# Rebuilding the front of a fused attention and feed-forward kernel on one core

## What is computed

```
x = x + attn_a(layernorm(x))     # q, k, v of width 1024, ONE head, causal softmax, w_o
x = x + ffn(layernorm(x))
x = x + attn_b(layernorm(x))     # 16 heads of 64, causal, own residual and own LayerNorm
x = x + ffn(layernorm(x))        # the same weights
ffn(x): s = x @ Win + bin                       # 64 units
        h = relu(s[..., None] * W1 + b1)        # 16 inner values per unit
        g = sum over the 16 of h * W2, + b2
        out = g @ Wout + bout
```

## Time and profile before

| | |
|---|---|
| median of 3 runs | 880.62 us (879.36 to 883.76) |
| profiled execution | 878.94 us, span 877.1 us |
| busy: TensorE, VectorE, ScalarE, GpSimd | 728.0, 665.4, 573.9, 520.9 us |
| start / front / back | 0 to 40.2 / to 226 / to 877.1 us |
| granted TensorE clock, mean | 0.923 |

### The profile page before, as it was taken

One profiled execution on the slowest core, in us unless ns is written; L12 is line 12 of the kernel. 1 busy time (PEld: TensorE's weight loads), 2 busy tenths in 40 slices (PEclk: granted clock), 3 DMA queues, 4 the chain that ended last, 5 costly groups with the idle time before them and its releaser, 6 DMA issues. The chain is left out here.

```text
span 877.1 us, 21234 instructions
## 1 busy us (share of the span) xinstructions
PE 728.0 (83%) x7592; PEld 523.7 (60%) x7592; DVE 665.4 (76%) x1358; ACT 573.9 (65%) x1575; POOL 520.9 (59%) x496
## 2 busy tenths in 40 slices
PE   4376666642689999999999999999999999998842
PEld 3265555532457676766767766766776676676531
DVE  2478888875466668868987996898799689879873
ACT  0257666653367676677777777777777777777633
POOL 2156666462156567766785685667578566766831
PEclk9599778865799999999999999999999999999985
DMA  9011111100079988899898888889889889898820
GB/s 210 23 48 49 49 48 37 48 25 36 25 131 150 152 146 141 147 144 140 143 146 137 150 139 145 145 141 144 138 151 143 142 143 141 151 143 152 147 58 24
DMA packets 367142, 100.29 MB, mean 114 GB/s; under 512 B 347968, under 2 KB 364864, under 8 KB 367040
## 3 DMA queue, kind: packets, MB, share of 16 engines
q1 hardware_dynamic: 363776, 96.86, 64.3%
q10 hardware_dynamic: 3264, 2.10, 0.9%
HBM read 8.73 MB, written 2.10 MB: 12 GB/s over the span
## 5 line engine op out<-in xcount | busy, mean ns | idle before, releaser
L1031 POOL TENSOR_TENSOR prob_hl<-prob,prob_hl 128x768 f16<-128x768 f32 (+1 forms) x192 | 347.5, 1810 | 205.3 <-DVE prob_hl L971 205.1
L942 ACT ACTIVATE prob<-wide,neg_max 128x128 f32<-128x128 f32 (+3 forms) x512 | 264.5, 525 | 155.6 <-DVE neg_max L983 155.5
L983 DVE TENSOR_REDUCE neg_max<-wide 128x2 f32<-128x256 f32 (+3 forms) x256 | 204.3, 819 | 109.9 <-PE wide L860 108.6
L855 PE MATMUL wide<-k_sb,q_sb 64*128 64x128 f32 (+3 forms) x1024 | 190.1, 469 | 0.9 <-ACT k_sb L837 0.8
L971 DVE CAST prob_hl<-prob 128x768 f16<-128x768 f32 (+1 forms) x192 | 155.1, 808 | 0.9 <-DMA prob_t<-prob_hl 0.7
L880 PE MATMUL bank<-v_hi,prob_t 128*128 128x64 f16 x1280 | 132.2, 193 | 15.4 <-DMA prob_t<-prob_hl 13.2
L882 PE MATMUL bank<-v_hi,prob_t 128*128 128x64 f16 x1280 | 132.2, 193 | 0.0
L881 PE MATMUL bank<-v_lo,prob_t 128*128 128x64 f16 x1280 | 132.2, 193 | 0.0
L880 PEld LDWEIGHTS bank<-v_hi,prob_t 128*128 128x128 f16 x1280 | 115.3, 98 | 21.4 <-issue 16.2
L882 PEld LDWEIGHTS bank<-v_hi,prob_t 128*128 128x128 f16 x1280 | 113.9, 98 | 0.0
L881 PEld LDWEIGHTS bank<-v_lo,prob_t 128*128 128x128 f16 x1280 | 113.8, 98 | 0.0
(11 more groups left out here) (190 smaller groups left out, 1427.0 us busy)
## 6 DMA issues: line engine op xcount, KB each, us to landing
prob_t<-prob_hl SPq DMA_TRANSPOSE x384, 3.2
x_next<-in_L_attn_a_in_features SPq DMA_DIRECT2D x8, 256.0 KB, 3.0
x_attn<-in_L_attn_a_in_features SPq DMA_DIRECT2D x8, 256.0 KB, 3.3
x_sb<-x_done SPq DMA_DIRECT2D x8, 256.0 KB, 2.3
y_res<-bn_y SPq DMA_DIRECT2D x8, 256.0 KB, 2.3
out_x<-x_done SPq DMA_DIRECT2D x8, 256.0 KB, 2.6
wq_a<-in_L_attn_a_w_q ACTq DMA_DIRECT2D x1, 512.0 KB, 5.3
wq_b<-in_L_attn_b_Wq SPq DMA_DIRECT2D x1, 512.0 KB, 8.4
```

The costliest lines, as they stand in the source:

```text
L855: pe.matmul(dst[:, h, c:c + m], q[e, i * P:(i + 1) * P], k[e, 0:m], start=(i == UNIT_ROWS[u][0]), stop=False)
L942: last = act.activation(prob_2[s][:, at:at + m], score_banks(p, s)[:, h, c:c + m], ACT.Exp, bias=neg_max[p % 2][:, h, i:i + 1], accum_out= ...
L983: last = dve.tensor_reduce(neg_max[p % 2][:, :, i:i + 1], score_banks(p, s)[:, :, c:c + m], AX.X, ALU.max, negate=True)
L1031: pool.tensor_tensor(prob_hl[u][:, w:2 * w], prob_2[u][:, 0:w], prob_hl[u][:, 0:w], ALU.subtract)\
```

## The change

- **Splits** are gone from the front, except that of `xt_hi` and `xt_lo`. Scores, `at_g`, the weighted values and the feed-forward's first product are single products of 4-byte operands; scores cover only the blocks up to the diagonal. ScalarE copies each operand once.
- **Feed-forward:** units 6 and 7 of each half are no longer summed on VectorE. Their `Relu`s stay; `ffn_out_pe` multiplies them with `w2_out`, which is `wout2` scaled by their `w2`, so the output product is 12 products in place of 4.
- **Order:** the turn of sequence `b - 3` (`bn`) stands on TensorE right behind the scores, ahead of the turning of the probabilities, and on ScalarE ahead of the first copy of these; on VectorE the residual `ffn_x_dve` stands first in the step and `bn`'s statistics behind the first row maximum.
- **Start:** all sequences are loaded once, straight into `x_sb`; the small feed-forward weights are loaded early, `attn_b`'s late. Sequence 0 is turned and its `at_g` made between the foldings. `vo_a` isn't scaled any more.
- **Weights of `attn_b`:** the largest value is found after step 2 (`scale_gpsimd`, an all-reduce over partitions on GpSimd), the scaling stands after step 7, the splits after step 8.
- `x_done`'s and `bn_y`'s copies by DMA are gone, and so is the hardware loop over steps.

The core of the diff:

```diff
+        def weighted_values(pe, u, v):
+
+            for k, (i, j) in enumerate(unit_blocks(u)):
+                last = pe.matmul(UO[:, i * P:(i + 1) * P], at_p_t[u][:, k * P:(k + 1) * P], v[:, j * P:(j + 1) * P],
+                                 start=(j == 0), stop=(j == i))
...
+        def load_tokens(sp, *bs):
+            for b in bs:
+                sp.dma_start(x_sb[:, seq(b), :], x_tiles[:, seq(b), :]).then_inc(sem(f"x_in{b}"), 16)
+
         def prepare_loads_sync(sp):
+            load_tokens(sp, 0)
+            sp.wait_ge(sem("b2_zeroed"), 1)
+            for dst, src in f_loads[:4]:
+                sp.dma_start(dst, src).then_inc(sem(LOADED_F), 16)
+            load_tokens(sp, 1)
+            for dst, src in f_loads[4:]:
+                sp.dma_start(dst, src).then_inc(sem(LOADED_F), 16)
+            load_tokens(sp, 2)
+            sp.wait_ge(sem(LOADED_A), 2 * 16)
+            load_tokens(sp, 3)
             for dst, src in b_loads:
                 sp.dma_start(dst, src).then_inc(sem(LOADED_B), 16)
-            sp.wait_ge(sem("b2_zeroed"), 1)
-            for dst, src in f_loads:
-                sp.dma_start(dst, src).then_inc(sem(LOADED_F), 16)
+            load_tokens(sp, *range(4, B))
 
...
+            pool.wait_ge(sem("const_0"), 7)
             front_gpsimd(pool, -2)
-            pool.wait_ge(sem("largest"), 2)
+            front_gpsimd(pool, -1)
+
+        def scale_gpsimd(pool):
+            pool.wait_ge(sem("largest"), 1)
             pool.partition_all_reduce(largest_all[:, :], largest[:, :], P, bass.bass_isa.ReduceOp.max)\
...
         def prepare_tensor(pe):
+            pe.wait_ge(sem("consts"), 3)
+            attn_turn_tensor(pe, 0)
             pe.wait_ge(sem(LOADED_QK_A), 2 * 16)
             for c in range(OC):
                 last = pe.matmul(bank[0][:, 0:P], wq_a[:, c, :], wk_a[:, c, :], start=(c == 0), stop=(c == OC - 1))
             last.then_inc(sem("qk_a_ps"), 1)
-            pe.wait_ge(sem("consts"), 3)
+            pe.wait_ge(sem("qk_a"), 1)
+            attn_g_tensor(pe, 0)
...
+            pe.wait_ge(sem("vo_a"), 1)
+            attn_v_tensor(pe, 0)
...
+            wait(pe, "f_xt", n + 1)
+            pe.matmul(bk[:, :], win2[:, :, :].rearrange("p a m -> p (a m)"), ffn_x[:, :], start=True, stop=True)\
                 .then_inc(sem("f_s_ps"), 1)
 
         def ffn_out_pe(pe, bk, n):
-            wait(pe, "f_add", J * n + J)
+            wait(pe, "f_relu", J * n + J)
+            wait(pe, "f_add", JA * n + JA)
             for i in range(QB):
-                last = pe.matmul(bk[:, i * P:(i + 1) * P], ffn_g[:, i * P:(i + 1) * P], wout2[:, :],
-                                 start=True, stop=True)
+                t = slice(i * P, (i + 1) * P)
+                pe.matmul(bk[:, t], ffn_g[:, t], wout2[:, :], start=True, stop=False)
+                for j in range(JA, J):
+                    last = pe.matmul(bk[:, t], ffn_relu[:, j % RELUS, t], w2_out[:, j - JA, :], start=False,
+                                     stop=(j == J - 1))
             last.then_inc(sem("f_o_ps"), 1)
...
         def ffn_relu_act(act, n, j):
             if j == 0:
                 wait(act, "f_s", n + 1)
-            wait(act, "f_add", J * n + max(j - RELUS + 1, 0))
+            if j >= RELUS:
+                wait(act, "f_add", JA * n + j - RELUS + 1)
+            elif (j + RELUS) >= JA:
+                wait(act, "f_o_ps", n)
+            else:
+                wait(act, "f_add", JA * (n - 1) + j + RELUS + 1)
...
+            dve.tensor_tensor(x_sb[:, seq(n), :], bk[:, :].rearrange("p (a d) -> p a d", d=P),
+                              ffn_xb[:, n % 2 * QB:(n % 2 + 1) * QB, :], ALU.add)\
                 .then_inc(sem("f_x2"), 1)
...
-                wait(sp, "f_x2", b - 2)
-                sp.dma_start(x_sb[:, seq(b - 3), :], x_done[:, :, :]).then_inc(sem("kept"), 16)
-                sp.wait_ge(sem("consts"), 3)
-                wait(sp, "bn_y", b - 2)
-                sp.dma_start(y_res[:, seq(b - 3), :], b_norm.y[:, :, :]).then_inc(sem("y_res_in"), 16)
-            if holds(b, -3, B - 4):
-                wait(sp, "at_y", b + 3)
-                sp.dma_start(x_next[:, :, :], x_tiles[:, seq(b + 3), :]).then_inc(sem("x_next_in"), 16)
...
-                    scores(pe, SC[u], u, at_g_hi, at_g_lo, at_x_hi, at_x_lo, 0).then_inc(sem("at_s"), 1)
+                    scores(pe, SC[u], u).then_inc(sem("at_s"), 1)
+            if attn_1:
+                wait(pe, "at_g", b + 1)
+                attn_turn_tensor(pe, b + 1)
+            if turn:
+                wait(pe, "bn_y", b - 2)
+                wait(pe, "f_x2", b - 2)
+                transposes(pe, FB, y_res[:, seq(b - 3), :].rearrange("p a d -> p (a d)"), QB)\
+                    .then_inc(sem("bn_xt_ps"), 1)
             if attn_2:
-                wait(pe, "at_p", NU * b + 1)
-                transposes(pe, TR[0], prob[0], len(unit_blocks(0))).then_inc(sem("at_pt"), 1)
+                for u in range(NU):
+                    wait(pe, "at_p", NU * b + u + 1)
+                    wait(pe, "at_pt", NU * b + u - 1)
+                    transposes(pe, TR[u % 2], prob[u], len(unit_blocks(u))).then_inc(sem("at_pt_ps"), 1)
             if attn_1:
...
+                attn_g_tensor(pe, b + 1)
+                attn_v_tensor(pe, b + 1)
+            if ffn_1:
+                ffn_project_pe(pe, SC[2], b - 1, before=[("at_p", NU * (b + 1)) if attn_2 else ("f_s", b - 1)])
             if attn_2:
-                wait(pe, "at_p", NU * b + 2)
...
-            if attn_1:
...
-                wait(pe, "at_x_lo", b + 2)
-                split_product(pe, GX[:, :], qk_a_hi[:, :], qk_a_lo[:, :], at_x_hi[:, :], at_x_lo[:, :])\
-                    .then_inc(sem("at_g_ps"), 1)
...
-                if attn_2:
-                    wait(pe, "at_pt_lo", NU * b + u + 1)
+                for u in range(NU):
...
-                    at = v_at(b)
-                    weighted_values(pe, lambda i: UO[:, i * P:(i + 1) * P], u,
-                                    lambda j: at_v_hi[:, bass.ds(at + j * P, P)],
...
-                if u == 1 and ffn_1:
-
-                    ffn_project_pe(pe, SC[2], b - 1, before=[("at_p", NU * (b + 1)) if attn_2 else ("f_s", b - 1)])
+                    weighted_values(pe, u, at_v[:, b % 2, :]).then_inc(sem("at_pv"), 1)
             if ffn_1:
                 ffn_s_pe(pe, SC[2], b - 1)
-            if turn:
-                wait(pe, "bn_y", b - 2)
-                transposes(pe, FB, b_norm.tokens(), QB).then_inc(sem("bn_xt_ps"), 1)
             if ffn_2:
                 wait(pe, "bn_xt_lo", b - 2)
                 ffn_out_pe(pe, FB, b - 2)
...
-            prob_t_scalar(0)
+            if attn_1:
+                attn_x_scalar(act, b + 1)
+            if turn:
+                wait(act, "bn_xt_ps", b - 2)
+                act.copy(xt_hi[:, (b - 3) * S:(b - 2) * S], FB[:, :]).then_inc(sem("bn_xt_hi"), 1)
+            turned(0)
...
-            if attn_1:
-                wait(act, "at_xt_ps", b + 2)
-                wait(act, "at_v_ps", b + 1)
-                act.copy(at_x[:, :], GX[:, :]).then_inc(sem("at_x"), 1)
-                wait(act, "at_s", NU * (b + 1))
-                act.copy(at_x_hi[:, :], GX[:, :]).then_inc(sem("at_x_hi"), 1)
-            prob_t_scalar(1)
-            prob_t_scalar(2)
+            turned(1)
+            turned(2)
...
-                wait(act, "at_v_ps", b + 2)
-                wait(act, "at_pv", NU * b)
-                act.copy(at_v_hi[:, bass.ds(v_at(b + 1), S)], SC[0][:, :]).then_inc(sem("at_v_hi"), 1)
-                wait(act, "at_g_ps", b + 2)
-                act.copy(at_g_hi[:, :], GX[:, :]).then_inc(sem("at_g_hi"), 1)
+                attn_g_scalar(act, b + 1)
+                attn_v_scalar(act, b + 1)
...
             if ffn_1:
-                ffn_xhi_act(act, SC[2], b - 1)
-            relus(6)
-            if turn:
-                wait(act, "bn_xt_ps", b - 2)
-                act.copy(xt_hi[:, bass.ds((b - 3) * S, S)], FB[:, :]).then_inc(sem("bn_xt_hi"), 1)
-            relus(7)
+                ffn_x_act(act, SC[2], b - 1)
+            relus(6, 7)
             if ffn_1:
                 ffn_s_act(act, SC[2], b - 1)
...
                     for j in js:
-                        ffn_add_dve(dve, b - 2, j)
-
-            def prob_t_vector(u):
...
-                    dve.tensor_tensor(prob_t_lo[u][:, 0:w], TR[u % 2][:, 0:w], prob_t_hi[u][:, 0:w], ALU.subtract)\
-                        .then_inc(sem("at_pt_lo"), 1)
-
+                        if j < JA:
+                            ffn_add_dve(dve, b - 2, j)
+
+            if turn:
+                ffn_x_dve(dve, FB, b - 3)
             for u in range(NU):
                 if attn_2:
                     wait(dve, "at_s", NU * b + u + 1)
                     row_maxima(dve, SC[u], u, at_neg_max).then_inc(sem("at_m"), 1)
+                if u == 0 and turn:
+                    wait(dve, "f_x2", b - 2)
```

(58 more changed lines are left out.)

245 lines of the change are left out of this document (99 added, 146 removed).

## The result

The changed kernel takes 876.03 us (median of 5, 874.36 to 876.4) where the kernel before takes 881.88 in the same session (median of 5, 879.36 to 884.7). The ratio is 0.9928, 95% interval 0.9912 to 0.9944: 0.7% faster, where 1.6% was forecast (866.5, range 855 to 881). The profiled execution took 875.58 us.

The account below looks back on a forecast made before the run. VectorE's list was taken to set the step before, a ring through the engines steps 3 to 7 after. -14.3 - 6.6 - 2.5 + 2.0 + 7.4 = -14.0 on 878.94 gave 864.9, stated as 866.5, range 855 to 881.

Parts of the forecast that it names:

- I take +2, near its own row: Steps 2 to 3: GpSimd's all-reduce, true cost between 0.38 and 16.9 us, was counted as +2 us.
- the ring: Steps 3 to 7: fn's apply, ffn_xb, bn's apply, turn, probabilities, weighted products, x_ffn and fn's statistics; 20.5 us a step.
- The rival of 15%: Steps 2 to 3: the all-reduce costs 10 us and more, total 875 to 882 us; chance 15%.
- the prediction's own sign against itself: Prediction is wrong if GpSimd stands still for more than 5 us behind the all-reduce.
- Start, -14.3: Start of the kernel: scores begin at 25.9 us in place of 40.2, 14.3 us earlier.
- Steps 0 to 2, -6.6: Steps without the turn: together 37.1 us where they took 43.7, 6.6 us less.
- Steps 3 to 7, 20.5 us each and 18.6 for step 7: Steps with the turn: 100.6 us in all against 103.1, 2.5 us less.
- the rival of the low clock through the whole run: TensorE's products: all at 1.2 GHz, together 28 us more, 894 us, so the kernel gets slower; chance 9%.
- The rule weighed: GpSimd's apply is shorter where VectorE is idle: five rings 0.4 to 0.8 us shorter each, total 861 to 863.
- The removed multiply-adds and subtractions are so worth nothing in these steps: Steps 3 to 7: some 6 us of VectorE's 17 a step go, but the ring covers them, so nothing is gained.
- Drain, +7.4: From the end of step 7: 46.4 us where it is 39.0, 7.4 us longer.
- The rival of the busiest engine: Steps 3 to 7: the busiest engine sets the time, say 14 us a step, total about 834; chance 5%.

## Why the prediction was right or wrong

**What failed is one term: "I take +2, near its own row" for the all-reduce in the ring.** It costs 13.3 us (left out, 13.3 less in step 3; used twice, 13.3 more in step 6). That is 11 us more than counted; the forecast for the profiled run was 864.9, and it took 875.58. The place was right, that it stands in the ring of steps 2 to 3, and the earlier trace rows gave the upper bound: 12.27 us of idle before the row, 16.50 behind. I chose the end that agreed with the duration of the row. The trace of before couldn't settle it, because both stretches also lie under waits for VectorE, whose results came at 21.58 and 38.44, just ahead of GpSimd's rows at 21.72 and 38.60:

```profile
21.29 0.29 DVE L283 TENSOR_REDUCE largest<-bank 128x1 f32<-128x128 f32 x1 [0.19 <-PE bank L255]
...
38.06 0.38 DVE L335 BATCH_NORM_AGGREGATE at_mean_var<-at_stats 128x2 f32<-128x6 f32 x4
```

The rival of 15% ("The all-reduce in the ring costs 10 us and more", 875 to 882) is what happened, and so did the prediction's own sign against itself, GpSimd standing still for more than 5 us behind the row (7.23). Two places of the Trainium skill would have spoken for it. GPSIMD Engine Reference (2.1 Instruction dispatch) says that the first call to a freshly loaded GpSimd kernel pays a load of about 6 us with no profile instruction to show for it; the traces agree, with 5.62 to 5.98 us ahead of the row, at the second use in a program too. The section has no price for what stands behind the row, which is 6.70 to 7.57 here; what GpSimd does then no run shows. Perfetto Trace Analysis (GPSIMD Engine Instruction) says to time GpSimd's instructions by the distance of their starts, not by the reported span; by starts its row in the trace of before is worth up to 16.9 us, the end that I did not take.

**Start, -14.3: it was -18.6.** Its working named the reason ("At the fast rate for the second half it would be 3 us less."): all products from `at_g` on ran at that rate, `at_g` and the eight turns in 1.12 and 1.04 us for 1.7 and 1.8, the fold of `vo_a` in 2.05 for 3.8, and `at_v` behind it in 1.16 for 1.9. The start passes to the end almost one to one (held back by 16.4, the end came 16.8 later).

**Steps 0 to 2, -6.6: they gave -2.4.** The parts were right in sum and the rate was not: at a clock of 1.00 they take 36.7 (forecast 37.1), with 0.87 and 0.79 in steps 1 and 2 41.2. That it cancels the start's error is luck.

**Steps 3 to 7, 20.5 us each and 18.6 for step 7: right, but for the all-reduce in step 3.** Steps 4 to 6 took 20.2 to 20.4 and step 7 18.7; the pause of 5 to 6 us, GpSimd's three pieces without a gap, VectorE idle for over a third, all as the prediction wished to see them. TensorE's ten weighted products ran at the full rate (2.40 us), so the rival of the low clock through the whole run did not come. (Its 5.5 us for the ring's own products should have been 5.7 to 5.9 by the prediction's terms, which changes nothing.) That a ring sets the steps is shown from two sides: 1.27 us out of it give 6.8 in all, and the turn one step later gives 31. Filling its pause gives 4.8, which shows what the clock adds to it.

**The rule weighed** (each ring 0.4 to 0.8 us shorter, because GpSimd is faster where VectorE is idle) is seen in the rows and not in the sum: the pass onto `y_res` takes 2.25 us in step 5, where a multiply-add runs beside it, and 1.76 in step 3, where VectorE is idle. But in steps 4 to 6 the multiply-add is there each time, and the ring came out 0.1 to 0.3 us under the 20.5.

**"The removed multiply-adds and subtractions are so worth nothing in these steps": wrong.** The two units alone are worth 6.8 us, since the ring's second half runs through VectorE too. The forecast didn't suffer, because it summed the branch that was in fact the longest, but it would have called moving the two units useless. The four loads and stores a step and the eight added products cost nothing that can be seen in the ring, though no run isolates them; with the ring gone the products are likely on the chain, since the scores moved ahead of them gave the fastest kernel.

**Drain, +7.4: right** (+7.0). **Back, 0:** it took 1.3 us longer. That says little: in the traces of the twelve other variants of the changed kernel the back takes 650.7 to 655.8 us.

**The rival of the busiest engine** (14 us a step, 834) was no description of this change. It is near what the last kernel comes to, with the ring taken out and the scores ahead of the output's products: 14.0 to 14.4 us a step and 821.82.

## What to carry to other kernels

Follow one unit of work through all engines' lists from a point back to the same point one step later: if that ring is as long as the step, work taken from the busiest engine returns little, and an order that hands a result to the next step rather than to this one returns much. Price an instruction by the distance between its neighbours' starts, above all on GpSimd, and put a dear one where its neighbours wait anyway. If in the only trace at hand such stretches also lie under other waits, its price is open, and the sum should say so. For TensorE's pauses look at what they cost twice, for themselves and for products at half rate behind them.
